# Half of the cross-attention weights turned through DRAM instead of by TensorE

## The chip, the cores and the metric

The kernel runs on one core of one Trainium2 chip. The metric is the device time of one execution in microseconds. A core has TensorE (matrix products, and transposes as products with an identity), VectorE, ScalarE, GpSimd, and SyncE, which here only issues DMAs; 16 DMA engines serve them.

## The reference

One post-norm decoder layer on 32 sequences of 56 tokens, 256 features, all in float32: self-attention, cross-attention to 1500 context positions, and a mixture of experts. The change lies in the middle part:

```
q = (text @ Wq), 16 heads of 128;  k, v = (ctx @ Wk), (ctx @ Wv), 8 heads, each used by two q heads
scores = q k^T / sqrt(128)                      # 16 x 56 x 1500 per sequence
attn = softmax(where(mask, scores, -inf))
x = layernorm(x + (attn v) @ Wo)
```

The kernel folds Wk into the queries and Wv into Wo (matrices M), so that the scores are products of the rotated queries with the context itself, and the weighted sum is one of context rows. A sequence (a *batch* of the attention) has 16 x 56 = 896 rows of weights, 7 *units* of 128 rows, and 1500 keys.

## The kernel before, in words

Phase A computes the self-attention and the rotated queries, phase C the experts; the change leaves both nearly as they are. Phase B is the cross-attention. Products are made exact to float32 by splitting each operand into a rounded part and a remainder (`_hi`, `_lo`, type fp32r) and adding three products: hi x hi, hi x lo, lo x hi.

Phase B goes over pairs of batches. The seven units of a batch stand in two slots, four units and then three; a slot has 12 *chunks* of 125 keys, and a pair has 48 steps, one per chunk. Per step every engine has its part, in an order written out by hand by step numbers:

- **fill** (TensorE L817 to L819): one third of a unit's scores, 128 x 500, into one of three score banks; VectorE (L983) adds the mask, takes the maximum and writes the row tile `p`; ScalarE (L901) takes exp of a whole unit of 1500 columns.
- **turn** (TensorE L831): the weighted sum needs the keys on the partitions, so each chunk of `p` (128 rows x 125 keys per unit) is turned into a PSUM bank, four transposes in an even slot, three in an odd one.
- ScalarE (L895) rounds the turned chunk to `pT_hi`, VectorE (L997) writes the remainder `pT_lo`.
- **weigh** (TensorE L850 to L852): three products of a chunk of context with `pT_hi` and `pT_lo`, 512 columns or 384, added up in an output bank over the 12 chunks.

Two batches' outputs are scaled by the reciprocal sums, rounded, and projected with M (L860, 48 products); then comes the layer norm. GpSimd splits queries, context and transposed context into hi and lo (L1099, L1101) and makes the mask's bias (L1110). SyncE loads `q_in`, `cT_in`, the mask and the context `c_in` for the batches ahead; ScalarE stores and loads the reciprocals. An engine does its instructions in order; a semaphore holds it where data or a buffer is missing. Matching rows of program and profile carry the same line number; the kernel's functions follow.

Of the kernel before, what the change touches and what calls it, by code (L numbers as in the profile page):

```python
# [26 lines left out]
ALU = mybir.AluOpType  # L27
# [21 lines left out]
CH = 12  # L49
CK = CTX // CH  # L50
FILLS = 3
FW = CTX // FILLS
ROWS = XH * S
UNITS = (4, 3)
SLOTS = 4
WIDE = UNITS[0] * 128
# [11 lines left out]
for width in (NT, EXPERTS * EXPERTS, 128, RP, RP, NT, NT * EXPERTS, 128):  # L68
# [8 lines left out]
Attention = namedtuple("Attention", "sync tensor scalar vector gpsimd edge tail q_split cT_split c_split fill_done fill_taken "  # L77
                       "first_batch_weighed weighed third_slot_turned all_lo projected z_taken y2_stored")
# [45 lines left out]
def phase_a(nc, D, semaphore, M_hi, M_lo, q_in, cT_in, ident, ident_loaded):  # L124
    with ExitStack() as ctx:
# [107 lines left out]
        def sync(sp, load_ahead):  # L233
# [56 lines left out]
            def store_last():  # L290
                store_q(NBLK - 1, range(PARTS))
                sp.wait_ge(y_stored, 16 * NPAIR)
                for part in range(PARTS):
                    sp.wait_ge(q_stored[part], 16 * NBLK)

            return store_last
# [331 lines left out]
def phase_b(nc, D, semaphore, edge, opening, M_hi, M_lo, q_in, cT_in, ident, const_loaded):  # L628
    with ExitStack() as ctx:
        def sb(name, shape, dt=F32):  # L630
            edge[name] = nc.sbuf_base
            return ctx.enter_context(nc.sbuf_tensor("b_" + name, shape, dt))

# [9 lines left out]

        oT = sb("oT", [128, XH, 2, S])
        oT_hi = sb("oT_hi", [128, XH, 2, S], F32R)
        oT_lo = sb("oT_lo", [128, XH, 2, S], F32R)
        y1_res = sb("y1_res", [PAIR, F])
# [4 lines left out]
        sb("spare", [128, 2480])  # L652
        pT_hi = sb("pT_hi", [CK, 3, WIDE], F32R)
        pT_lo = sb("pT_lo", [CK, 3, WIDE], F32R)
        p = [None, sb("p1", [128, UNITS[1], CTX])]
        rden_all = sb("rden_all", [128, 2, WIDE])
# [6 lines left out]
        c_in = sb("c_in", [CK, CH * CD])  # L663
        c_hi = sb("c_hi", [CK, 2, CH * CD], F32R)
        c_lo = sb("c_lo", [CK, 2, CH * CD], F32R)
        mask_in = sb("mask_in", [128, CTX], U8)
        mask_add = sb("mask_add", [128, 2, CTX], BF16)
        half = sb("half", [PAIR, 1])
        top = sb("top", [128, 2, UNITS[0], FILLS + 1])
        top_min = sb("top_min", [128, FILLS + 1])  # L670
        shift = sb("shift", [128, 2, UNITS[0]])
        den = sb("den", [128, 2, UNITS[0]])
        rden = sb("rden", [128, 2, UNITS[0]])
        p[0] = sb("p0", [128, UNITS[0], CTX])
        edge["end"] = nc.sbuf_base
# [3 lines left out]
        q_loaded, cT_loaded, c_loaded, mask_loaded = sem("q_loaded"), sem("cT_loaded"), sem("c_loaded"), sem("mask_loaded")  # L679
# [29 lines left out]
        def units(slot):  # L709
            return UNITS[slot % 2]  # L710
# [1454 lines left out]
```

## Time and profile before

| | |
|---|---|
| median of 3 runs | 1717.78 us (1717.73 to 1717.91) |
| span of the profiled execution | 1718.6 us |
| its own time outside the span | not given apart; the span is 0.8 us above the median |
| mean granted clock of TensorE | 0.994 of 2.4 GHz |
| DMA, mean over the span | 82 GB/s |

The span goes from the first to the last instruction of one profiled execution. A share of an engine is its busy time over the span. In the tables of stretches, DMA share is the mean busy share of the 16 DMA engines. In the chain of waits, followed back from the end, each piece is the time that TensorE (or another) spent as the last to be ready. Rows of instruction groups give the busy time in all and the mean duration of one in ns; a matmul's mean duration overlaps its neighbours, so for TensorE the chain's pieces tell the pace.

### The profile page before, as it was taken

The numbers are of one execution on the slowest core, as the hardware profiler recorded it, in microseconds if no ns is written. First come the engines' busy times: TensorE is split into PE (matmuls) and PEld (weight loads), VectorE is DVE, ScalarE is ACT, GpSimd is POOL, SyncE is SP. The second block draws the span as 40 slices with busy tenths as digits, with TensorE's granted clock in tenths as the row PEclk, the third lists the DMA queues.
The fourth block names the chain that finished last, engine by engine and source line by source line (L and its number), as shares of the span: only waits on it lengthen the run. The fifth ranks groups of instructions, "written<-read, shape, count | busy, mean of one in ns | idle before, by whom it ended". The sixth has DMA issues, their size and how long they took to land.

```text
span 1718.6 us, 28903 instructions
## 1 busy us (share of the span) xinstructions
PE 1685.0 (98%) x10034; PEld 1517.0 (88%) x10034; DVE 1221.3 (71%) x3377; ACT 937.2 (55%) x1717; POOL 664.6 (39%) x417
## 2 busy tenths in 40 slices
PE   7999999999999999999999999999999999999996
PEld 7998889898989898989898989989898989888985
DVE  5655676877787878777778777776878787756557
ACT  5444465656565656565656565565656565644543
POOL 1220344525243333333334343443525341355435
PEclk9999999999999999999999999999999999999998
DMA  5234643423141423333232323232324130431433
GB/s 197 81 132 130 193 95 78 70 68 81 54 97 41 90 44 88 48 86 68 62 68 63 68 63 68 70 66 77 74 61 89 52 57 12 112 114 40 121 90 95
DMA packets 102856, 140.29 MB, mean 82 GB/s; under 512 B 37022, under 2 KB 81728, under 8 KB 102592
## 3 DMA queue, kind: packets, MB, share of 16 engines
q1 hardware_dynamic: 60784, 115.47, 26.8%
q10 hardware_dynamic: 38912, 14.80, 4.0%
q0 software_dynamic: 3024, 8.26, 1.8%
q8 instruction: 79, 1.29, 0.4%
q14 instruction: 57, 0.47, 0.2%
HBM read 113.62 MB, written 24.89 MB: 81 GB/s over the span
## 4 chain that ended last, share of the span: by engine, by line
PE 93%; DVE 2%; issue 1%; ACT 1%; DMA 1%; POOL 0%; another core or an unknown queue 0%; POOLq 0%; SPq 0%; ACTq 0%; DVEq 0%
PE b_turn L831 17%; PE b_out L850 9%; PE b_out L851 9%; PE b_out L852 9%; PE b_score L817 9%; PE b_score L819 9%; PE b_score L818 9%; PE b_out L860 5%; PE a_bank L344 5%; PE c_gate L1513 2%; PE c_down L1540 1%; PE a_bank L370 1%; PE a_bank L395 1%; PE a_bank L424 1%; PE a_bank L417 1%
## 5 line engine op out<-in xcount | busy, mean ns | idle before, releaser
L895 ACT CAST b_pT_hi<-b_turn 125x512 fp32r<-125x512 f32 (+1 forms) x768 | 406.8, 530 | 543.0 <-PE b_turn L831 539.8
L997 DVE TENSOR_TENSOR b_pT_lo<-b_turn,b_pT_hi 125x512 fp32r<-125x512 f32 (+1 forms) x768 | 478.0, 623 | 259.7 <-ACT b_pT_hi L895 254.2
L983 DVE CUSTOM_DVE_ANT_0 b_p<-b_score,b_mask_add 128x500 f32<-128x500 f32 x672 | 451.9, 673 | 58.9 <-PE b_turn L831 24.4
L831 PEld LDWEIGHTS b_turn<-ident,b_p 128*125 128x125 f32 x2688 | 409.4, 186 | 55.2
L831 PE MATMUL b_turn<-ident,b_p 128*125 128x128 f32 x2688 | 418.1, 272 | 0.0
L901 ACT ACTIVATE b_p<-b_p,b_shift 128x1500 f32<-128x1500 f32 x224 | 347.5, 1551 | 2.1 <-DVE b_top_min L991 2.1
L850 PE MATMUL b_out<-b_pT_hi,b_c_hi 125*128 125x512 f32 (+1 forms) x768 | 346.5, 451 | 0.7 <-DVE b_pT_lo L997 0.6
L1135 POOL TENSOR_TENSOR b_oT_lo<-b_oT,b_oT_hi 128x896 fp32r<-128x896 f32 x32 | 67.6, 2112 | 624.5 <-ACT b_oT_hi L925 588.0
L851 PE MATMUL b_out<-b_pT_lo,b_c_hi 125*128 125x512 f32 (+1 forms) x768 | 280.9, 366 | 0.0
L852 PE MATMUL b_out<-b_pT_hi,b_c_lo 125*128 125x512 f32 (+1 forms) x768 | 280.5, 365 | 0.0
L817 PE MATMUL b_score<-b_cT_hi,b_q_hi 128*128 128x500 f32 x672 | 262.9, 391 | 0.0
L819 PE MATMUL b_score<-b_cT_hi,b_q_lo 128*128 128x500 f32 x672 | 260.2, 387 | 0.0
L818 PE MATMUL b_score<-b_cT_lo,b_q_hi 128*128 128x500 f32 x672 | 259.8, 387 | 0.0
L852 PEld LDWEIGHTS b_out<-b_pT_hi,b_c_lo 125*128 125x128 f32 x768 | 144.2, 188 | 17.9
L819 PEld LDWEIGHTS b_score<-b_cT_hi,b_q_lo 128*128 128x128 f32 x672 | 126.1, 188 | 25.8
L850 PEld LDWEIGHTS b_out<-b_pT_hi,b_c_hi 125*128 125x128 f32 x768 | 145.7, 190 | 1.5 <-DVE b_pT_lo L997 1.4
L851 PEld LDWEIGHTS b_out<-b_pT_lo,b_c_hi 125*128 125x128 f32 x768 | 145.9, 190 | 0.0
L818 PEld LDWEIGHTS b_score<-b_cT_lo,b_q_hi 128*128 128x128 f32 x672 | 128.1, 191 | 14.2
L817 PEld LDWEIGHTS b_score<-b_cT_hi,b_q_hi 128*128 128x128 f32 x672 | 126.2, 188 | 14.1
L1101 POOL TENSOR_TENSOR b_c_lo<-b_c_in,b_c_hi 125x1536 fp32r<-125x1536 f32 x32 | 111.9, 3497 | 2.7
L1101 POOL TENSOR_TENSOR b_cT_lo<-cT_in,b_cT_hi 128x1500 fp32r<-128x1500 f32 x31 | 106.3, 3428 | 2.6
L860 PE MATMUL b_out<-M_lo,b_oT_hi 128*112 128x256 f32 x256 | 71.8, 280 | 0.0
(250 smaller groups left out, 2402.1 us busy)
## 6 DMA issues: line engine op xcount, KB each, us to landing
cT_in<-in_ctxT SPq DMA_DIRECT2D x32, 750.0 KB, 9.8
b_c_in<-in_ctx SPq DMA_DIRECT2D x32, 750.0 KB
q_store<-a_fold_in_or_q_stage SPq DMA_DIRECT2D x16, 896.0 KB, 4.2
q_in<-q_store SPq DMA_DIRECT2D x32, 448.0 KB, 7.1
b_rden_all<-rden_store ACTq DMA_DIRECT2D x32, 256.0 KB, 3.6
b_rden_all<-rden_store ACTq DMA_DIRECT2D x32, 192.0 KB, 3.7
b_mask_in<-in_mask SPq DMA_DIRECT2D x32, 187.5 KB, 9.4
slot_store<-c_y2T SPq DMA_DIRECT2D x35, 128.0 KB, 1.7
```

The lines of the kernel that those rows point to most:

```text
L817: pe.matmul(out, q_hi[b][:, rows], cT_hi[b][:, keys], start=True, stop=False)
L818: pe.matmul(out, q_hi[b][:, rows], cT_lo[b][:, keys], start=False, stop=False)
L819: pe.matmul(out, q_lo[b][:, rows], cT_hi[b][:, keys], start=False, stop=True).then_inc(fill_done, 1)
L831: mm = pe.transpose(turn_bank[n % 3][0:CK, u * 128:(u + 1) * 128], p[slot % 2][:, u, c * CK:(c + 1) * CK], ident[:])
L850: pe.matmul(out, hi, pT_hi[:, n % 3, 0:w], start=(c == 0), stop=False)
L851: pe.matmul(out, hi, pT_lo[:, n % 3, 0:w], start=False, stop=False)
L852: pe.matmul(out, lo, pT_hi[:, n % 3, 0:w], start=False, stop=(c == CH - 1)).then_inc(pv_done, 1)
L895: act.copy(pT_hi[:, n % 3, 0:w], turn_bank[n % 3][0:CK, 0:w]).then_inc(hi_done, 1)
L901: act.activation(row, row, ACT.Exp, bias=shift[:, slot % 2, u:u + 1], scale=float(X_SCALE), accum_out=den[:, slot % 2, u:u + 1]).then_inc( ...
L983: dve.tensor_tensor_reduce(out=p[slot % 2][:, u, keys], in0=score_bank[j][:, 0:FW], in1=mask_add[:, b, keys], scale=1.0, scalar=-3.0e38, o ...
L997: dve.tensor_tensor(pT_lo[:, n % 3, 0:w], turn_bank[n % 3][0:CK, 0:w], pT_hi[:, n % 3, 0:w].bitcast(F32), ALU.subtract).then_inc(lo_done, 1)
L1101: pool.tensor_tensor(lo, src, hi.bitcast(F32), ALU.subtract).then_inc(done, 1)
```

## The change

Units are now worked by single batches: 24 steps (`STEPS = 2 * CH`) for one batch's seven units. The odd slot's three units are turned by TensorE as before. The four even units of a batch take another way:

1. VectorE (`turn_blocks`) turns the unit's 128 x 1536 values in 32 x 32 blocks into the one buffer `by_block`, at steps 5, 9, 13 and 17. It reads the row so that 32 keys (padded beyond 125) of each of 12 chunks and four quarters (`al`) come as blocks.
2. SyncE stores `by_block` to DRAM (`store_p`), 6144 B for each of 128 rows.
3. When a batch's four units are stored, SyncE fetches them (`load_keyed`): for each unit and each quarter `a` of its rows a band of 384 columns into `keyed`, with the keys on the partitions. The source is read as 4 quarters of keys x 32 x 384 values; the target is 128 partitions x 384 values. `keyed` is a single buffer; the fetch waits until the even products of the batch before are done.
4. ScalarE (`keyed_round`) rounds a chunk of 512 columns, GpSimd (`keyed_rest`) writes the remainder over `keyed`, and TensorE (`weigh_even`) multiplies, twelve chunks later than the odd units' products.

To make room, the remainders of the context and of the scaled output are written over their sources, `p0` holds three units, and the residual is loaded into `z`. The casts of `cT` and `c` go from GpSimd to ScalarE (`cT_round` at step 1, `c_round` at step 8). The projection is cut into four parts of 12 products. In phase C tiles move to other regions; two shared-expert weights are loaded only when the attention's products are done.

```diff
+        STEPS = 2 * CH
...
+        HI_AT = STEPS + 2
+        PV_AT = HI_AT + 2
+        BLOCKS_AT = (5, 9, 13, 17)
+        RDEN_AT, STORE_AT, LOAD_AT = (15, STEPS + 1), (16, STEPS + 2), (STEPS + 16, STEPS + 8)
+        SCALE_AT = (PV_AT + STEPS - 1, PV_AT + CH - 1)
+        ROUND_AT = SCALE_AT[0] + 1
...
+            def store_p(m, u):
+                sp.wait_ge(blocks_turned, EVEN * m + u + 1)
+                if m >= 2:
+                    sp.wait_ge(keyed_loaded, 16 * QUADS * EVEN * (m - 1))
+                sp.dma_start(D["p"][m % 2, u].rearrange("q a n -> q (a n)"),
+                             by_block[:].rearrange("q al b j -> q (al b j)")).then_inc(p_stored, 16)
+            def load_keyed(m, u):
+                if m:
+                    sp.wait_ge(pv_done, whole(m - 1))
+                sp.wait_ge(p_stored, 16 * EVEN * (m + 1))
+                for a in range(QUADS):
+                    sp.dma_start(keyed[:, QUADS * u + a, :],
+                                 D["p"][m % 2, u, 32 * a:32 * (a + 1)].rearrange("i al n -> al i n")).then_inc(keyed_loaded, 16)
...
+            for m in range(B):
+                if m >= 2:
+                    load_c(m)
+                if m:
+                    store_p(m, 0)
+                    for u in range(EVEN):
+                        load_keyed(m - 1, u)
+                if m + 2 < B:
+                    load_q(m + 2)
+                if m:
+                    store_p(m, 1)
+                store_p(m, 2)
+                if m + 2 < B:
+                    load_cT(m + 2)
+                    load_mask(m + 2)
+                store_p(m, 3)
...
-                for u in range(units(slot)):
-                    mm = pe.transpose(turn_bank[n % 3][0:CK, u * 128:(u + 1) * 128],
-                                      p[slot % 2][:, u, c * CK:(c + 1) * CK], ident[:])
+                for u in range(ODD):
+                    mm = pe.transpose(turn_bank[c % 3][0:CK, u * 128:(u + 1) * 128],
+                                      p[1][:, u, c * CK:(c + 1) * CK], ident[:])
...
+                pe.wait_ge(keyed_lo_done, CH * m + c + 1)
+                out, (hi, lo) = by_blocks(out_bank[0][:]), values(m, c)
+                own_hi = by_blocks(pT_hi[:, c % 3, :])
+                pe.matmul(out, hi, own_hi, start=(c == 0), stop=False)
+                pe.matmul(out, hi, keyed_chunk(keyed_lo, c), start=False, stop=False)
+                pe.matmul(out, lo, own_hi, start=False, stop=(c == CH - 1)).then_inc(pv_done, 1)
...
+            def keyed_round(m, c):
+                if c == 0:
+                    act.wait_ge(keyed_loaded, 16 * QUADS * EVEN * (m + 1))
+                act.wait_ge(pv_done, STEPS * m + CH + c - 2)
+                act.copy(by_blocks(pT_hi[:, c % 3, :]), keyed_chunk(keyed, c)).then_inc(hi_done, 1)
...
+            def turn_blocks(m, u):
+                dve.wait_ge(exp_done, PUNITS * m + u + 1)
+                dve.wait_ge(p_stored, 16 * (EVEN * m + u))
+                own = row(m, u)
+                keys = bass.AP(own.tensor, own.offset, [own.ap[0], [32, QUADS], [CK, CH], [1, 32]])
+                dve.transpose(by_block[:], keys).then_inc(blocks_turned, 1)
...
+            def keyed_rest(m, c):
+                pool.wait_ge(hi_done, STEPS * m + CH + c + 1)
+                pool.tensor_tensor(keyed_chunk(keyed_lo, c), keyed_chunk(keyed, c),
+                                   by_blocks(pT_hi[:, c % 3, :]).bitcast(F32),
+                                   ALU.subtract).then_inc(keyed_lo_done, 1)
...
+    D["p"] = nc.dram_tensor("p_store", (2, EVEN, 128, QUADS, ACROSS), F32, kind="Internal").ap()
```

TensorE, an even slot in the steady state: the scores of a fill (`b_score`), then one chunk, its turn (`b_turn`) and its products (`b_out`). Before:

```order
L817 MATMUL b_score2<-b_cT_hi0,b_q_hi0 128x500
L818 MATMUL b_score2<-b_cT_lo0,b_q_hi0 128x500
L819 MATMUL b_score2<-b_cT_hi0,b_q_lo0 128x500
L831 MATMUL b_turn1<-ident,b_p0 125x128 x4
L850 MATMUL b_out0<-b_pT_hi,b_c_hi 128x512
L851 MATMUL b_out0<-b_pT_lo,b_c_hi 128x512
L852 MATMUL b_out0<-b_pT_hi,b_c_lo 128x512
```

After, the same stretch of work (`b_keyed_over` is the remainder written over `keyed`, `b_c_raw1_over` that of the context over its source):

```order
L864 MATMUL b_score0<-b_cT_hi0,b_q_hi0 128x500 [waits b_fill_taken]
L865 MATMUL b_score0<-b_cT_lo0,b_q_hi0 128x500
L866 MATMUL b_score0<-b_cT_hi0,b_q_lo0 128x500
L912 MATMUL b_out0<-b_pT_hi,b_c_hi1 128x512 [waits b_keyed_lo_done]
L913 MATMUL b_out0<-b_keyed_over_50,b_c_hi1 128x512
L914 MATMUL b_out0<-b_pT_hi,b_c_raw1_over_52 128x512
```

The four transposes are gone; the first product waits for the remainder of the fetched chunk.

SyncE's queue, one batch. Before:

```order
L750 ISA [waits b_q_split]
L750 DMA q_in<-q_store 128x896
L756 ISA [waits b_cT_split]
L756 DMA cT_in<-in_ctxT 128x1500
L759 DMA b_mask_in<-in_mask 128x1500
L766 DMA b_c_in<-in_ctx 125x1536 [waits b_c_split]
```

After (`p_store` is the DRAM tensor of step 2; where rows are left out, the same four rows of `b_keyed` stand three times more, 16 fetches in all):

```order
L786 DMA b_c_raw0<-in_ctx 125x1536 [waits b_pv_done]
L792 DMA p_store<-b_by_block 128x1536 [waits b_keyed_loaded,b_blocks_turned]
L802 DMA b_keyed<-p_store 128x1x384 [waits b_p_stored,b_pv_done]
L802 DMA b_keyed<-p_store 128x1x384 x3
...
L772 DMA q_in<-q_store 128x896 [waits b_q_split]
L792 DMA p_store<-b_by_block 128x1536 [waits b_keyed_loaded,b_blocks_turned] x2
L776 DMA cT_in<-in_ctxT 128x1500 [waits b_cT_lo_done]
L781 DMA b_mask_in<-in_mask 128x1500 [waits b_mask_ready]
L792 DMA p_store<-b_by_block 128x1536 [waits b_keyed_loaded,b_blocks_turned]
```

Between the load of `c` and that of `q_in` stand a store and sixteen fetches; the stores of the second, third and fourth unit come behind them in the same queue.

VectorE, scores (`b_p`, `b_top`) and remainders (`b_pT_lo`). Before:

```order
L991 TENSOR_SCALAR b_top_min,b_shift<-b_top 128x4 [waits b_fill_taken]
L997 TENSOR_TENSOR b_pT_lo<-b_turn0,b_pT_hi 125x512 [waits b_hi_done]
L997 TENSOR_TENSOR b_pT_lo<-b_turn1,b_pT_hi 125x512 [waits b_hi_done]
L983 ISA b_p1,b_top<-b_score0,b_mask_add 128x500 [waits b_fill_done]
L983 ISA b_top 128x1
L997 TENSOR_TENSOR b_pT_lo<-b_turn2,b_pT_hi 125x512 [waits b_hi_done]
```

After, around the block transpose of one unit (step 9):

```order
L1067 ISA b_top 128x1
L1076 TENSOR_SCALAR b_top_min,b_shift<-b_top 128x4 [waits b_fill_taken]
L1091 TENSOR_TENSOR b_pT_lo<-b_turn1,b_pT_hi 125x384 [waits b_hi_done]
L1086 STREAM_TRANSPOSE b_by_block<-b_p0 128x1536 [waits b_p_stored,b_exp_done]
L1067 ISA b_p0,b_top<-b_score0,b_mask_add 128x500 [waits b_blocks_turned,b_fill_done]
L1067 ISA b_top 128x1
L1091 TENSOR_TENSOR b_pT_lo<-b_turn2,b_pT_hi 125x384 [waits b_hi_done]
```

The remainders have 384 columns; a transpose of 1536 columns stands between scores and waits until the store of the unit before has landed.

## Rows read from the trace of the kernel before

**Rows 1.** The page: busy us (share) x instructions, and the chain that ended last by line.
```profile
PE 1685.0 (98%) x10034; PEld 1517.0 (88%) x10034; DVE 1221.3 (71%) x3377; ACT 937.2 (55%) x1717; POOL 664.6 (39%) x417
...
PE b_turn L831 17%; PE b_out L850 9%; PE b_out L851 9%; PE b_out L852 9%; PE b_score L817 9%; PE b_score L819 9%; PE b_score L818 9%; PE b_out L860 5%; PE a_bank L344 5%; PE c_gate L1513 2%; PE c_down L1540 1%; PE a_bank L370 1%; PE a_bank L395 1%; PE a_bank L424 1%; PE a_bank L417 1%
```
**Rows 2.** Stretches: busy us and instructions by engine, granted clock, DMA share, GB/s.
```profile
174.60:256.50 81.90, 81.90 (x434) 72.80 (x435) 59.72 (x161) 42.97 (x69) 33.15 (x17) 0.98 0.58 143
256.50:1485.60 1229.10, 1229.10 (x7292) 1108.02 (x7291) 925.64 (x2656) 711.52 (x1171) 487.23 (x249) 1.00 0.31 69
1485.60:1519.70 34.10, 33.40 (x225) 30.44 (x224) 19.06 (x36) 19.96 (x36) 22.11 (x26) 1.00 0.09 22
```
**Rows 3.** The chain in order of time: start us, us, what; two projections.
```profile
949.65 5.62 PE b_out L860 x48
1031.60 5.62 PE b_out L860 x48
```
**Rows 4.** The chain, single chunks of four and of three units.
```profile
989.80 0.23 PE b_score L817
...
990.48 0.44 PE b_turn L831 x4
990.91 0.23 PE b_out L850
...
1301.38 0.33 PE b_turn L831 x3
1301.70 0.18 PE b_out L850
```
**Rows 5.** Groups of 256.5:1485.6: shapes, count | busy us, mean ns | idle before.
```profile
L983 DVE CUSTOM_DVE_ANT_0 b_p<-b_score,b_mask_add 128x500 f32<-128x500 f32 x630 | 423.7, 672 | 48.7 <-PE b_turn L831 23.6 <-PE b_score L819 6.5
...
L997 DVE TENSOR_TENSOR b_pT_lo<-b_turn,b_pT_hi 125x512 fp32r<-125x512 f32 x361 | 248.9, 689 | 180.2 <-ACT b_pT_hi L895 176.8
...
L997 DVE TENSOR_TENSOR b_pT_lo<-b_turn,b_pT_hi 125x384 fp32r<-125x384 f32 x360 | 200.1, 556 | 65.9 <-ACT b_pT_hi L895 64.6 <-issue 0.5
...
L895 ACT CAST b_pT_hi<-b_turn 125x384 fp32r<-125x384 f32 x360 | 171.3, 476 | 219.4 <-PE b_turn L831 219.4
...
L1101 POOL TENSOR_TENSOR b_c_lo<-b_c_in,b_c_hi 125x1536 fp32r<-125x1536 f32 x30 | 104.9, 3497 | 2.5
...
L1135 POOL TENSOR_TENSOR b_oT_lo<-b_oT,b_oT_hi 128x896 fp32r<-128x896 f32 x29 | 61.3, 2113 | 561.7 <-ACT b_oT_hi L925 561.7
...
L1099 POOL TENSOR_SCALAR b_c_hi<-b_c_in 125x1536 fp32r<-125x1536 f32 x30 | 44.5, 1483 | 0.0
...
L1099 POOL TENSOR_SCALAR b_cT_hi<-cT_in 128x1500 fp32r<-128x1500 f32 x29 | 42.1, 1452 | 0.0
```
**Rows 6.** Stretches of single transfers: c, c, storing q (phase A), cT.
```profile
1032.40:1038.40 6.00, 6.00 (x50) 5.85 (x49) 0.09 (x1) 0.71 (x2) 0.00 (x0) 1.00 0.29 116
950.50:956.50 6.00, 6.00 (x50) 5.83 (x49) 0.13 (x1) 0.75 (x2) 0.00 (x0) 1.00 0.31 122
...
76.70:78.70 2.00, 2.00 (x11) 1.73 (x10) 0.62 (x1) 0.28 (x1) 0.00 (x0) 1.00 1.01 333
...
1002.30:1005.10 2.80, 2.80 (x18) 2.51 (x17) 2.29 (x6) 1.64 (x4) 0.36 (x1) 1.00 0.93 330
```
**Rows 7.** DMA issues: out<-in, queue, count, KB each, median us to landing.
```profile
q_in<-q_store SPq DMA_DIRECT2D x32, 448.0 KB, 7.1
b_rden_all<-rden_store ACTq DMA_DIRECT2D x32, 256.0 KB, 3.6
b_rden_all<-rden_store ACTq DMA_DIRECT2D x32, 192.0 KB, 3.7
...
slot_store<-c_y2T SPq DMA_DIRECT2D x35, 128.0 KB, 1.7
```
**Rows 8.** Stretches where phase B begins.
```profile
171.00:174.60 3.60, 1.36 (x11) 0.91 (x10) 1.85 (x6) 1.91 (x4) 0.08 (x1) 1.00 0.79 195
174.60:178.10 3.50, 3.50 (x10) 3.09 (x11) 3.50 (x2) 1.77 (x2) 1.36 (x1) 0.51 0.80 287
178.10:182.00 3.90, 3.90 (x20) 3.53 (x20) 1.84 (x5) 0.54 (x1) 2.57 (x2) 1.00 0.97 332
```

More of the change, by code:

```diff
@@ new lines, in fills_at, with unit_ends, parity, behind @@
+        def fills_at(n):
+            return [f for f in range(PFILLS) if fill_step(f) == n]
+        def unit_ends(n, late):
+            return [f // FILLS for f in range(FILLS - 1, PFILLS, FILLS) if fill_step(f) + late == n]
+        def parity(u):
+            return (0, u) if u < EVEN else (1, u - EVEN)
+        def behind(m, n, at, count=1):
+            for k in range(3):
+                if at <= n + STEPS * k < at + count and 0 <= m - k:
+                    return m - k, n + STEPS * k - at
+            return None
@@ new lines, in units_behind, with row, whole, keyed_chunk @@
+        def units_behind(m, n, late, last):
+            ends = [] if last else [(m, u) for u in unit_ends(n, late)]
+            return ends + ([(m - 1, u) for u in unit_ends(n + STEPS, late)] if m else [])
+        def row(m, u):
+            return p[0][:, (EVEN * m + u) % EVEN_DEEP, :] if u < EVEN else p[1][:, u - EVEN, :]
+        def whole(m):
+            return STEPS * (m + 1)
+        def keyed_chunk(tensor, c):
+            return tensor[0:CK, :, 32 * c:32 * (c + 1)]
+        def by_blocks(ap):
+            return ap.rearrange("p (g j) -> p g j", j=32)
@@ L797, in sync @@
-            loads(1, first=True)
-            with sp.Fori(2, NPAIR) as i:
-                loads(i)
-            store(NPAIR - 2)
-            residual(NPAIR - 1)
+                load_mask(0)
+                load_c(0)
+            store_last_part, wait_stored = opening.sync(sp, load_ahead)
+            load_q(1)
+            load_cT(1)
+            load_mask(1)
+            load_c(1)
+            for part in range(len(opening.stored)):
+                if part >= 2:
+                    store_p(0, part - 2)
+                store_last_part(part)
@@ L854, in project @@
[L854 to L857 removed]
+                    if m == 0:
+                        pe.wait_ge(*opening.taken[1])
+                    else:
+                        pe.wait_ge(oT_done, OT_OPS * (2 * m - 1))
+                    pe.wait_ge(c_lo_done, m + 1)
+                pe.wait_ge(lo_done, CH * m + c + 1)
+                out, (hi, lo) = out_bank[1][:, 0:w], values(m, c)
+                pe.matmul(out, hi, pT_hi[:, c % 3, 0:w], start=(c == 0), stop=False)
@@ L861, in project @@
                                        start=(h == 0 and n == 0), stop=(h == XH - 1 and n == len(terms) - 1))
[L862 to L878 removed]
+                if part == parts - 1:
+                    mm.then_inc(proj_done, 1)
```

773 lines of the change are left out of this document (388 added, 385 removed).

## The prediction

> **What bounds the kernel now.** I read the page's busy shares first, then the chain of waits, then a table by stretches. TensorE is busy 98% of the span, the next engine 71% [rows 1]; the chain that ends last is TensorE for 93%, its largest line the turning L831 with 17% [rows 1]. In the attention proper, from 174.6 us to 1485.6 us, TensorE never idles: 81.90 of 81.90 us in the first pair of batches, 1229.10 of 1229.10 us in the fifteen that follow [rows 2]. A pair recurs every 81.95 us (the projection L860 starts at 949.65 and at 1031.60) [rows 3], so a batch takes 40.97 us. What this kernel does in the attention is the sum of TensorE's instructions; all else is hidden, DMA included (mean share 0.31, 69 GB/s) [rows 2].
>
> **What the change takes from TensorE.** In the chain a chunk of four units is turned in 0.44 us, one of three in 0.33 us [rows 4]. Twelve chunks of four per batch go: 12 x 0.44 = 5.28 us, and over 32 batches 169 us. The order shows nothing put in their place on TensorE: the even chunk's three products follow the scores directly. If all else stayed hidden, a batch would take 40.97 - 5.28 = 35.7 us.
>
> **What the other engines get, against 35.7 us a batch.** GpSimd is busy 487.23 us in thirty batches [rows 2], 16.2 us each. It gives the casts of c and cT to ScalarE (1.48 and 1.45 us) and gets twelve remainders of 512 columns. None is in the trace; 896 columns take 2113 ns and 1536 take 3497 ns [rows 5], 2.16 ns a column and some 180 ns besides, so 1.29 us each, 15.4 us a batch. That makes 28.7 us. It fits, and one remainder per step of 1.49 us (35.7 / 24) fits as well, barely; up to double is possible, since these tiles are cut into pieces of 32 columns, and would make GpSimd the bound at 44 us a batch. VectorE, busy 925.64 / 30 = 30.9 us a batch [rows 2], loses twelve remainders of 512 columns (689 ns [rows 5], 8.3 us) and gains four block transposes of 1536 columns. No row shows that operation. 384 and 512 columns take 556 and 689 ns [rows 5], 1.04 ns a column, which makes 1.75 us each, 7.0 us a batch; I bound it by 0.9 us (half) and 3.5 us (double) and take 1.75, the line through the nearest rows: 29.6 us. ScalarE, 711.52 / 30 = 23.7 us now [rows 2], gets the casts of cT and c, some 3 us more. By these values no engine becomes the bound by its work.
>
> **What the DMA gets.** Per batch and unit, one store of 128 rows x 6144 B (768 KB, four a batch) and four fetches of 128 x 1536 B (192 KB, sixteen a batch): 3 MB out and 3 MB back. The question is how many of the 16 DMA engines a fetch uses. In two windows in which only the load of c runs (125 rows), the DMA share is 0.29 and 0.31, with 116 and 122 GB/s; in a window of the load of cT (128 rows) it is 0.93 and 330 GB/s, and 1.01 and 333 GB/s where q is stored (128 rows) [rows 6]. 0.31 is 5/16: 125 rows are split by 5, and 128 by 16. So a transfer is cut along its outermost count into equal parts. The fetch of a band reads its source as 4 x 32 x 384 (al, i, n): the outermost count is 4, against 128 partitions on the other side. Cut the same way it runs on 4 engines.
> Here the Trainium skill has a rule that speaks against this change: "DMA: Bandwidth & Descriptors", section "Why a DMA increments its semaphore by 16 and not by 1", says that a hardware-issued transfer gets the largest number of engines, up to 16, that divides the slowest dimension of both sides. By that rule the trace's 0.31 for 125 rows is 5 engines, and agrees; a band gets 4. No transfer here has unlike counts on its two sides, so this half of the rule is not shown by any row. By the rule the sum is the one below; if only the 128 partitions counted, it would be that of the first rival.
> Four engines carry 786,432 B each per batch for the fetches. One engine moves 122 / 5 = 24.4 GB/s, 330 / (0.93 x 16) = 22.2 or 333 / (1.01 x 16) = 20.6 [rows 6]; I take 23.
>
> **The cycle of one batch.** SyncE's order is: store of unit 0, sixteen fetches of the batch before, q, store of unit 1, then store of unit 2. All go through one queue, so on the four engines the store of unit 1 stands behind the fetches. VectorE has one by_block buffer: its transpose of unit 2 (end of step 13) waits until unit 1 is stored, and behind it on VectorE, in order, stand all later scores; TensorE, with three score banks, stops at the fill of step 18. ScalarE's first rounding of the fetched bands (step 14) waits for the same fetches. So, from the issue of unit 0's store:
> 1. On each of the four engines: 2 x 49,152 B of stores, 786,432 B of bands, 28,672 B of q and as much of rden (448 KB each a batch [rows 7]), 942,080 B; at 23 GB/s 41.0 us. Issue and receipt 1.7 us (a 128 KB store lands in 1.7 us [rows 7]). The load of c, issued two steps earlier, is mostly through. 42.7 us.
> 2. Transpose of unit 2, 1.75 us, and the next score, 0.67 us [rows 5]: 2.5 us with the shift between them.
> 3. TensorE from step 18 to step 5 of the next batch. Its parts: a fill 3 x 0.225, products of 512 columns 3 x 0.23, of 384 3 x 0.175, a turn of three 0.33 [rows 4]. Five steps of 1.37, step 23 at GpSimd's 1.29, two of 1.37, two of 1.70, two of 1.53: 17.3 us.
> 4. From TensorE's end of step 5 to the end of the next unit 0's transpose: cast 0.48 and remainder 0.56 of three units [rows 5], transpose 1.75, less 0.5 beside TensorE: 2.3 us.
> 5. TensorE has then stood still for about 30 us. After it idled for 2.2 of 3.6 us, the trace shows a stretch of 3.5 us at granted clock 0.51, the lower of its two levels, 1.2 GHz, and 1.00 again after it [rows 8]. Half of such a stretch is lost at most, 1.7 us, part of it in waits: 1.2 us.
> Sum 66.0 us a batch, against 40.97.
>
> **The sum.** The profiled span is 1718.6 us, 0.8 above the median of the timed runs, 1717.8; what lies around the span is below what I can resolve here. Outside the attention's sixteen pairs 1718.6 - 1311.0 = 407.6 us stay. Batch 0 has no fetch: 35.7. Batches 1 to 31: 31 x 66.0 = 2046. At the end the last batch's fetch has no work beside it but some twelve light steps: 34 us of fetch and then the twelve chunks, against 34.1 us from the end of the pairs to the last projection now [rows 2]; I add 30 us, and 5 us for two shared-expert weights that the last stage now loads only when the attention's buffers are free (0 to 15). 407.6 + 35.7 + 2046 + 35 = 2524 us. For its own range the engine's rate gives 38.6 us (24.4) to 45.7 us (20.6) in term 1, the transpose -1.7 to +3.5 us, the queueing of c up to +5 us, term 5 0 to 1.7: with not all ends at once 60 to 75 us a batch, 2340 to 2805 us. GpSimd at double would lengthen term 3, in which eleven of its twelve remainders lie, by up to 11 us; with the low end of the rest that still is within the range.
>
> **The rivals.**
> First, and on the other side: the fetch is cut by its 128 partitions and uses all 16 engines. For it speaks that every 128-row transfer of the trace does; against it the 5 of 125, which show that counts decide. Then term 1 is (2 x 49,152 + 196,608 + 28,672) B at 20.6 GB/s, 15.7 us, + 1.7 = 17.4 us, and VectorE arrives at its wait after TensorE's steps 6 to 13, 7 fills of 0.675 and 8 x 0.855, 11.6 us. Of the 5.8 us late, TensorE's lead covers some 2: 39.7 us a batch, 407.6 + 35.7 + 31 x 39.7 + 10 = 1684 us. The point from which it decides: a batch gets slower than 40.97 us when the sixteen fetches take over some 11 us, that is with fewer than about 14 engines at this rate.
> Second: the fetches are hidden altogether and TensorE stays the bound: 407.6 + 32 x 35.7 + 10 = 1560 us. It needs the rival above and 6 us less of DMA.
> Third: four engines, but the waits overlap and only their occupancy counts. Per batch they carry 786,432 + 196,608 (stores) + 153,600 (c, a fifth of it) + 48,000 (cT) + 28,672 (q) + 12,000 (mask) + 28,672 (rden) = 1,253,984 B, at 23 GB/s 54.5 us: 407.6 + 35.7 + 31 x 54.5 + 35 = 2168 us. Against it: the by_block buffer is single and VectorE takes its work in order.
> That the change doesn't do what it says is excluded by the order.
>
> **How the numbers follow.** The forecast 2524 us has 0.76, the third rival 0.06, the first 0.11, the second 0.07. The range reaches from below the third rival to the upper end of the forecast's own: 2150 to 2820. Faster by over 0.2% (about what a measurement can tell here) are the first and second, less a little: 0.17; within 0.2% 0.01; slower 0.82.
>
> **What would show it.** Right: fetches of b_keyed landing over 30 us after issue; DMA share near 0.25 for most of a batch; VectorE idle some 28 us a batch before the transpose of by_block, released by the store of p; TensorE's share of the attention near 55%, L878 at three units only; a project line every 132 us. A half-speed clock after each stall would show term 5. Wrong: a DMA share of 0.8 or more while b_keyed is fetched, and a batch under 41 us. If the share is 0.25 and the time is not near 2524, a term of the cycle is mis-sized: the rate, or what stands behind what.

## The result, and the profile after

The changed kernel takes 2716.58 us (median of 4 runs, 2715.55 to 2726.51), the kernel before 1717.76 beside it: ratio 1.583 [1.580, 1.585]. The forecast was 2524 with a range of 2150 to 2820; the direction and the mechanism hold, and the size is 193 us short.

The page of the changed kernel: span, busy us (share) x instructions, then the chain that ended last, by engine and by line.

```profile
span 2713.7 us, 26254 instructions
...
PE 1691.3 (62%) x8498; PEld 1444.2 (53%) x8498; DVE 1189.1 (44%) x3134; ACT 1019.4 (38%) x1780; POOL 1038.2 (38%) x726
...
DMA 29%; SPq 26%; PE 17%; DVE 10%; ACT 4%; issue 3%; POOL 2%; DVEq 0%; ACTq 0%; POOLq 0%
SPq L802 24%; DMA p_store<-b_by_block 17%; DMA b_c_raw<-in_ctx 11%; DVE b_by_block L1086 5%; ACT b_p L971 2%; SPq L772 2%; PE b_out L912 2%; PE b_score L864 2%; PE b_score L866 2%; PE b_score L865 2%; DVE b_p L1067 2%; POOL b_keyed_over L1238 2%; PE b_turn L878 1%; PE c_gate L1632 1%; PE b_out L913 1%
```

TensorE was the chain for 93% [rows 1] and is now 17% of it. In its place stand SyncE's issuing of the fetches (L802, 24%), the landing of p's stores (17%) and, at 11%, the load of c, of which the prediction had said that it is mostly through.

The table of waits of the same kernel: who waited for whom, us in total, times, longest.

```profile
DVE b_by_block L1086 <- DMA p_store<-b_by_block: 867.3, 65, 28.5
PE b_out L912 <- POOL b_keyed_over L1238: 789.6, 100, 25.8
...
ACT b_pT_hi L964 <- DMA b_keyed<-p_store: 698.1, 31, 24.7
```

VectorE's transposes wait 65 times for the one by_block buffer. Some 800 of the 867.3 us fall before unit 2's transpose, up to 28.5 us each; the rest is a shorter wait before unit 3's, which the prediction does not have. ScalarE's first rounding of the bands waits 31 times, once a batch, up to 24.7 us. The waits at unit 2 and at the rounding are the two of the prediction's cycle.

Stretches of the changed kernel (busy us by engine, granted clock, DMA share, GB/s), as [rows 2]: the thirty batches' stretch of before, then one in which only bands are fetched, then the five microseconds behind an issue of c's load.

```profile
256.50:1485.60 1229.10, 701.59 (x3316) 589.94 (x3315) 506.00 (x1380) 449.07 (x701) 488.17 (x314) 0.79 0.48 127
...
1340.00:1345.00 5.00, 0.00 (x0) 0.00 (x0) 0.00 (x0) 0.00 (x0) 0.00 (x0) 0.50 0.27 100
...
1304.40:1309.70 5.30, 5.30 (x34) 4.97 (x33) 5.17 (x13) 4.21 (x7) 2.72 (x2) 1.00 0.19 22
```

TensorE is busy 57% where it was busy 100%. A band's fetch alone runs at share 0.27, 100 GB/s: four engines of sixteen, 25 GB/s each. All compute stands still there, and the clock is granted at its lower level (0.50, 1.2 GHz). The third row is the surprise: c's load is under way, and 22 GB/s move. In the kernel before, the same load moved 91 and 96 GB/s in the 5.3 us behind its issue (two batches), and 116 to 122 once it ran [rows 6].

SyncE's timeline over one batch (start us, us; a piece is a run of one kind of issue), and pieces of the chain of the same batch:

```profile
1238.53 0.33 SPq L792 DMA_DIRECT2D p_store<-b_by_block  x1
1238.96 32.83 SPq L802 DMA_DIRECT2D b_keyed<-p_store  x16
1271.83 1.83 SPq L772 DMA_DIRECT2D q_in<-q_store  x1
```
```profile
1273.76 10.63 DMA p_store<-b_by_block
...
1284.48 1.79 DVE b_by_block L1086
```

Sixteen issues hold SyncE for 32.83 us. The first two take 0.5 and 0.7 us, most of the later ones 1.86 us, about what one band's 196,608 bytes need at 100 GB/s; that an issue there waits for room in a full queue is read from this, not shown by a row. Unit 1's store, written behind them, lands at 1284.39, 45.9 us after unit 0's store was issued. Transposes of unit 2 start at 1213.27, 1284.48 and 1355.69: 71.2 us a batch, 71.4 over all 31, where the forecast had 66.0.

Groups of the page of after (busy us, mean ns | idle before) for the operations that no row of before showed:

```profile
L1238 POOL TENSOR_TENSOR b_keyed_over<-b_keyed,b_pT_hi 125x512 fp32r<-125x512 f32 x372 | 466.9, 1282 | 1051.2 <-ACT b_pT_hi L964 1051.2
...
L1086 DVE STREAM_TRANSPOSE b_by_block<-b_p 128x1536 f32<-128x1536 f32 x128 | 227.0, 1774 | 867.3 <-DMA p_store<-b_by_block 867.3
```

1282 ns against the 1.29 us forecast, 1774 against 1.75.

### The profile page after: what moved, and what is told of

It is laid out like the page before. It is cut to its first block, busy times and chain, and to the rows that moved or that the text cites. A ratio compares the mean times of both kernels' runs of the same rounds, so it can differ in the third digit from the quotient of the medians.

```text
span 2713.7 us, 26254 instructions
## 1 busy us (share of the span) xinstructions
PE 1691.3 (62%) x8498; PEld 1444.2 (53%) x8498; DVE 1189.1 (44%) x3134; ACT 1019.4 (38%) x1780; POOL 1038.2 (38%) x726
## 3 DMA queue, kind: packets, MB, share of 16 engines
q1 hardware_dynamic: 146800, 316.81, 41.5%
q10 hardware_dynamic: 38912, 14.80, 3.0%
## 4 chain that ended last, share of the span: by engine, by line
DMA 29%; SPq 26%; PE 17%; DVE 10%; ACT 4%; issue 3%; POOL 2%; DVEq 0%; ACTq 0%; POOLq 0%
SPq L802 24%; DMA p_store<-b_by_block 17%; DMA b_c_raw<-in_ctx 11%; DVE b_by_block L1086 5%; ACT b_p L971 2%; SPq L772 2%; PE b_out L912 2%; PE b_score L864 2%; PE b_score L866 2%; PE b_score L865 2%; DVE b_p L1067 2%; POOL b_keyed_over L1238 2%; PE b_turn L878 1%; PE c_gate L1632 1%; PE b_out L913 1%
## 5 line engine op out<-in xcount | busy, mean ns | idle before, releaser
L1238 POOL TENSOR_TENSOR b_keyed_over<-b_keyed,b_pT_hi 125x512 fp32r<-125x512 f32 x372 | 466.9, 1282 | 1051.2 <-ACT b_pT_hi L964 1051.2
L912 PE MATMUL b_out<-b_pT_hi,b_c_hi 125*128 125x512 f32 x384 | 186.1, 485 | 792.6 <-POOL b_keyed_over L1238 789.6
L1086 DVE STREAM_TRANSPOSE b_by_block<-b_p 128x1536 f32<-128x1536 f32 x128 | 227.0, 1774 | 867.3 <-DMA p_store<-b_by_block 867.3
L964 ACT CAST b_pT_hi<-b_keyed 125x512 fp32r<-125x512 f32 x384 | 218.8, 613 | 873.0 <-DMA b_keyed<-p_store 698.1
L1091 DVE TENSOR_TENSOR b_pT_lo<-b_turn,b_pT_hi 125x384 fp32r<-125x384 f32 x384 | 213.0, 556 | 294.0 <-ACT b_pT_hi L957 288.0
L957 ACT CAST b_pT_hi<-b_turn 125x384 fp32r<-125x384 f32 x384 | 179.8, 477 | 270.6 <-PE b_turn L878 266.3
L896 PE MATMUL b_out<-b_pT_hi,b_c_hi 125*128 125x384 f32 x384 | 167.7, 437 | 136.9 <-DVE b_pT_lo L1091 136.9
L878 PEld LDWEIGHTS b_turn<-ident,b_p 128*125 128x125 f32 x1152 | 193.9, 195 | 29.4
L878 PE MATMUL b_turn<-ident,b_p 128*125 128x128 f32 x1152 | 195.7, 280 | 0.0
L913 PE MATMUL b_out<-b_keyed_over,b_c_hi 125*128 125x512 f32 x384 | 167.1, 435 | 0.0
```

Source lines behind the costliest of these rows:

```text
L878: mm = pe.transpose(turn_bank[c % 3][0:CK, u * 128:(u + 1) * 128], p[1][:, u, c * CK:(c + 1) * CK], ident[:])
L896: pe.matmul(out, hi, pT_hi[:, c % 3, 0:w], start=(c == 0), stop=False)
L912: pe.matmul(out, hi, own_hi, start=(c == 0), stop=False)
L964: act.copy(by_blocks(pT_hi[:, c % 3, :]), keyed_chunk(keyed, c)).then_inc(hi_done, 1)
L1086: dve.transpose(by_block[:], keys).then_inc(blocks_turned, 1)
L1238: pool.tensor_tensor(keyed_chunk(keyed_lo, c), keyed_chunk(keyed, c), by_blocks(pT_hi[:, c % 3, :]).bitcast(F32), ALU.subtract).then_inc(k ...
```

## The experiments

Each ratio is given with its 95% interval against the kernel before (1717.5 to 1718.6 us). The time a batch is the mean distance of unit 2's transposes over batches 2 to 31, by which the changed kernel has 70.97 us.

**More engines for the same bytes.** The fetch in 4 transfers a batch, each into 32 partitions, with an outermost count of 32:

```
-  for a in range(QUADS):
-      sp.dma_start(keyed[:, QUADS*u + a, :], D["p"][m % 2, u, 32*a:32*(a+1)].rearrange("i al n -> al i n"))
+  sp.dma_start(keyed[32*u:32*(u+1), :, :], D["p"][m % 2, :, :, u].rearrange("v (a i) n -> i (v a) n", i=32))
```

> The same bytes in the same packets of 1536 B, fetched in four transfers per batch, one per quarter of 32 keys' partitions, whose outermost count is 32 on both sides, in place of sixteen with counts 4 and 128. Theory (a fetch is cut along its outermost count, 4 engines): all 16 engines carry it, the fetch takes some 9 us instead of the 32 us of the trace (1320 to 1352 us), DMA share 0.8 or more in it. The cycle was 71.2 us = 10.3 us from the store's issue to the first band + 32 + 3.6 + 25.2; it becomes 10.3 + 9 + 3.6 + 25.2 = 48 us, or less where the wait for c overlaps: 44 to 48 us, 1820 to 1950 us in all. Rival A (the pass through DRAM itself, 3 MB out and back with its waits, is the cost, whatever the number of engines): within 5% of 2717 us. Rival B (SyncE's issues are the cost, 24% of the chain): four issues instead of sixteen would help as much, so this run does not tell it from the theory; e2_eight does.

Measured 2320.5 us, 1.352 [1.349, 1.355], 58.9 us a batch. The count decides how many engines take part, but 16 of them bring less than four times the rate. The same cut in pieces of 8 partitions, so that 8 engines take part:

```
+  for k in range(QUADS): at = 8*k
+      sp.dma_start(keyed[32*u+at:32*u+at+8, :, :], D["p"][...].rearrange("v (a i) n -> i (v a) n", i=32)[at:at+8])
```

> Sixteen transfers of 192 KB per batch as before, same packets, but each takes 8 partitions and the source is read with an outermost count of 8. Theory: 8 engines, a fetch of 16 us instead of 32, DMA share near 0.5 in it, 55 us a batch, 2717 - 32 x 16 = 2205 us. Rival B (SyncE's sixteen issues at 1.86 us are the cost and not the engines): 2717 us, issues still 1.86 us apart. Rival A (the pass through DRAM): 2717 us.

Measured 2540.7 us, 1.479 [1.469, 1.489], 64.3 us a batch. The rivals of both runs, the pass through DRAM as such and SyncE's sixteen issues, had no change here, and are out. Stretches in which the bands are fetched, first of the 8-engine version, then of the 16-engine one (in the latter little else moves):

```profile
1190.00:1202.00 12.00, 8.01 (x43) 7.69 (x44) 5.87 (x14) 4.62 (x7) 3.48 (x1) 0.72 0.54 124
```
```profile
1260.00:1264.00 4.00, 2.06 (x6) 1.89 (x7) 2.67 (x3) 3.58 (x6) 3.00 (x1) 0.50 1.08 214
```

Share 0.27, 0.54, 1.08, but 100, 124, 214 GB/s: in the records of single packets between 600 and 1400 us, a packet of 1536 bytes takes 65 ns on the mean on 4 engines, 99 on 8 and 126 on 16. Both expectations had taken the rate per engine as given and were too low. From its first packet to its last, the fetch took 32.4 us in the changed kernel, 31.8 on 8 engines and 25.8 on 16 (means over batches 2 to 30). Of the 6.7 and 12.1 us a batch that the two versions win, some 6 come from the start: the first packet starts 3.9 and 4.0 us behind unit 0's store instead of 10.0, before c has landed. In the waits of the 16-engine version a new one is large:

```profile
ACT b_c_hi L1002 <- DMA b_c_raw<-in_ctx: 368.8, 30, 14.2
```

ScalarE casts c at step 8, in order before the exponentials of the units behind it, and c's load, issued at step 3 at the earliest, is not there: 12.3 us a batch. In the changed kernel the same wait was 229.7 us.

**c's load and the order of the queue.** In the changed kernel, c in two transfers of 112 and 13 rows:

```
-  sp.dma_start(c_raw[m % 2][:], D["ctx"][m])
+  for rows in (slice(0, 112), slice(112, CK)): sp.dma_start(c_raw[m % 2][rows, :], D["ctx"][m, rows, :])
```

> Only the load of c (125 rows, 5 engines) is cut into 112 and 13 rows. In the trace the first band starts 10.3 us after the store of unit 0 is issued, where 2.8 us were reckoned. Theory: c's 25 packets on each of the first five engines stand ahead of the fetch; with 7 + 1 packets the start comes some 5 us earlier, 66 us a batch, about 2560 us. Rival (c is through in time, the late start is the store of p or slow packets of all kinds): 2717 us within 15.

Measured 2641.2 us, 1.538 [1.535, 1.541]: 75 us less, between the two. c still took 11.4 to 11.7 us on the chain, so its five engines were only part of it. And unit 1's store ahead of the sixteen fetches:

```
   store_p(m, 0)
+  store_p(m, 1)
   for u in range(EVEN): load_keyed(m - 1, u)
```

> Only SyncE's order: the store of unit 1 stands ahead of the sixteen fetches, which so start at step 9 instead of 5, with c's load long done. Theory (what counts is the fetch's 32 us plus all the steps that can't go on beside it): VectorE's wait moves from unit 2's transpose to unit 3's and ScalarE's wait for the bands ends last; 36 us from unit 1's store to the bands + 29.6 us from step 14 to step 9 = 65.6 us a batch, 2540 us. Rival (the single by_block buffer behind the fetches is the cost by itself): once unit 1's store is ahead, most of the wait goes, under 2200 us; or, if the store of unit 2 only takes its place, 2717 us.

Measured 2897.1 us, 1.687 [1.683, 1.691], slower, and both expectations fell. VectorE's wait for the single buffer fell from 867.3 to 15.9 us, and still the time grew. SyncE waits for the transpose at step 9 before it issues any fetch, and that transpose stands behind ScalarE's wait for c: the first band starts 16.6 us behind unit 0's store instead of 10.0, and a batch takes 76.9 us. Its row of waits for the bands (the changed kernel has 698.1 and 24.7):

```profile
ACT b_pT_hi L963 <- DMA b_keyed<-p_store: 942.2, 31, 32.5
```

The fetch itself has to be early; the store's place behind it was the smaller evil.

**What slows c.** In the packet records of the changed kernel between 600 and 1400 us, a 6144-byte packet takes 234 ns in the median, but 918 ns on the mean when it starts 5 to 7 us behind an issue of the reciprocals' store, and up to 5.3 us singly. That store writes 512 and 384 pieces of 4 bytes, the second at step 2, right before c's load. One edit in the changed kernel makes it 128 pieces of 12 or 16 bytes, and leaves the order in DRAM unlike the one that the load expects, so that rows are scaled by other rows' sums:

```
-  D["rden"][m, par, 0:128*u].rearrange("(u q) -> q u", q=128)
+  D["rden"][m, par, 0:128*u].rearrange("(q u) -> q u", u=u)
```

> The changed kernel with one edit: the reciprocals of a batch go to DRAM as one piece of 16 or 12 bytes for each of 128 rows instead of 512 and 384 pieces of 4 bytes (their order in DRAM is then another, so the outputs are scaled by wrong denominators; the time alone counts). Theory: the 4-byte pieces slow every transfer beside and behind them for some microseconds (packets of 6144 bytes 234 ns each away from them, up to 2 us right behind them), c's load, issued just behind them, takes 15 us instead of 7, and the bands wait behind c: the load of c falls to 8 us, 5 to 7 us a batch come back, 2717 falls to 2500-2560. Rival: the slow packets come from something else that falls into the same steps: 2717 +- 15 and c still takes 15 us.

Measured 2571.2 us, 1.497 [1.494, 1.500]; 66.5 us a batch. The waits, and the five microseconds behind an issue of c's load:

```profile
ACT b_c_hi L1003 <- DMA b_c_raw<-in_ctx: 88.5, 30, 6.0
```
```profile
1235.60:1240.90 5.30, 5.30 (x34) 4.98 (x33) 5.17 (x13) 4.21 (x7) 2.72 (x2) 1.00 0.23 64
```

ScalarE waits 88.5 us for c, in the changed kernel 229.7; 64 GB/s move where 22 did; packets 5 to 7 us behind the issue take 237 ns instead of 918. The bytes differ by nothing that counts (14.80 MB on that queue in both), only the pieces. SyncE's sixteen issues take 28.6 us instead of 32.9 on the mean. The cycle of both kernels in parts (us, means over batches 2 to 30, from the packet records):

| | changed kernel | larger pieces |
|---|---|---|
| unit 0's store to the first band's packet | 10.0 | 5.0 |
| first to last band | 32.4 | 33.1 |
| last band to unit 2's transpose | 3.4 | 3.4 |
| from there to the next unit 0's store | 25.2 | 25.2 |

The whole gain is the earlier start of the bands. This is the theory's outcome, a little short of its range.

**Where the data lie.** Each unit stored in 4 transfers, by block of queries, so that it comes back in one transfer with an outermost count of 128:

```
+  for a in range(QUADS):
+      sp.dma_start(D["p"][m % 2, u, a].rearrange("(al i) n -> i al n", i=32), by_block[32*a:32*(a+1)]...)
...
+  sp.dma_start(keyed[:, QUADS*u:QUADS*(u+1), :], D["p"][m % 2, u].rearrange("a p n -> p a n"))
```

> The changed kernel with another layout in DRAM: each unit is stored in 4 transfers of 32 partitions, each block of queries apart, so that a unit is fetched back by one transfer whose outermost count is 128 (4 transfers a batch, all 16 engines, all 128 partitions at once, still 1536 bytes a packet). In the version with 4 transfers of 32 partitions the packets took 110 to 130 ns on 16 engines and 2320 us in all. Theory 1: those packets were slow because each transfer wrote to 32 partitions alone; with 128 partitions they take 65 to 80 ns, the fetch 10 us instead of 15, and the time falls to 2150-2220. Theory 2: 16 engines with packets of 1536 bytes end at some 200 GB/s however the partitions lie: 2320 +- 40, packets of 110 ns or more.

Measured 2296.3 us, 1.338 [1.336, 1.341]: by the time alone the second theory's number. Its own waits say otherwise:

```profile
ACT b_c_hi L1003 <- DMA b_c_raw<-in_ctx: 266.1, 30, 11.6
```

c is late here as well, 8.9 us a batch, and may cover what the fetch wins. The 16-engine version of before with c in two transfers:

> The version that fetches in 4 transfers of 32 partitions (2320 us), with c's load in two transfers of 112 and 13 rows, so that its rows go over 14 engines instead of 5. Theory: c's load, 20 us from issue to landing, is the wait that ScalarE's cast at step 8 has in that version (25% of the chain), because its packets stand in 5 queues; spread it takes 12 to 14 us and 4 to 6 us a batch go: 2130-2200. Rival: what holds c is the writes of other transfers that all engines share, and 2320 moves by no more than the 75 us that the same edit brought with 4 engines.

Measured 2149.3 us, 1.251 [1.246, 1.255]. 171 us for the edit that brought 75 with 4 engines; the theory's range. Then layout, split c and pieces of 12 or 16 bytes together:

> All three edits together: the layout with fetches of 128 partitions, c in two transfers, and the reciprocals stored in one piece a row (which leaves their order in DRAM wrong, the time alone counts). If the three costs are the three that hold the version with 4 transfers of 32 partitions (2320 us), they leave 1850-2000 us, still above the 1718 before, because store and fetch of 6.3 MB a batch at some 250 GB/s need 25 us of the 41 and the fetch can begin only when the last product of the batch before is done. If DRAM traffic as such bounds it, 2150 or more.

Measured 1925.0 us, 1.121 [1.119, 1.123], 46.4 us a batch, within the theory's range. A stretch of it in which the fetch runs, with part of q's load beside it:

```profile
1180.00:1187.00 7.00, 7.00 (x51) 6.73 (x50) 4.51 (x15) 1.70 (x4) 2.54 (x1) 1.00 1.05 395
```

395 GB/s, 342 of them bands, at 65 ns a packet in the median, against 214 for transfers into 32 partitions with the same packet size on the same 16 engines. So theory 1 of the layout was right on the packets. Whether the partitions or the order of the reads in DRAM does it, these runs don't part: the edit changes both. What is left on the chain is `DMA p_store<-b_by_block` with 29%, the single buffer; VectorE waits 319.8 us for it.

**Toward a version that beats both.** The layout and the split c stay. The reciprocals are turned by VectorE and stored in their right order as 28 pieces of 128 bytes, by_block has two buffers, and the fetch goes first.

```
-  act.dma_start(D["rden"][m, par, ...].rearrange("(u q) -> q u"), rden[:, par, 0:u])
+  dve.transpose(rden_t[:], rden[:])
+  for a in range(4): act.dma_start(D["rden"][m].rearrange("(u a j) -> a u j", a=4, j=32)[a], rden_t[32*a:32*a+7, :])
...
-  EVEN_DEEP = 3;  by_block = sb("by_block", ...)
+  EVEN_DEEP = 2;  by_block = [sb(f"by_block{k}", ...) for k in range(2)]
...
-  load_c(m); store_p(m, 0); load_keyed(m - 1, ...)      C_HI_AT = 8
+  load_keyed(m - 1, ...); load_c(m); store_p(m, 0)      C_HI_AT = 12
```

> A version meant to beat both, whose outputs are the reference's: units stored in 4 transfers by block of queries and fetched by transfers of 128 partitions; c in two transfers; the reciprocals of a batch turned by VectorE (one 128x32 transpose) and stored as 28 pieces of 128 bytes instead of 896 of 4; two buffers for the turned unit (the ring of even units one shorter), so that a transpose waits for the store two units back; and the fetch issued ahead of c's load and of unit 0's store, with c's cast moved from step 8 to step 12. Theory: what remains in the version with the first three (1925 us) is the wait of the transpose for the store (29% of the chain), which the second buffer ends, and the late start of the fetch (8.5 us at 65 ns a packet, wanted at step 14, free to begin at step 3). Then TensorE sets the pace with 12 turns of 4 units (5.3 us) fewer than before: 36 to 39 us a batch against 41, 1560 to 1660 us. Rival: DRAM traffic of 9.5 MB a batch, with stores in packets of 1536 bytes at 100 ns, still makes SyncE's queue late for the cast at step 14: 42 us a batch or more, 1750 or more.

Measured 1728.1 us, 1.0058 [1.0042, 1.0075]: between theory and rival. With fetches into 32 partitions instead:

> The same, but with the layout of the change: units stored in one transfer with packets of 6144 bytes, the fetch in 4 transfers of 32 partitions, whose packets took 110 to 130 ns in the first such version. If the fetch's speed decides (15 us against 8.5), this is slower by up to 5 us a batch, 1700 to 1800; if its 18 us of room cover it, it is as fast as the other within 20 us, or faster, since the stores are cheaper.

Measured 1910.4 us, 1.112 [1.110, 1.114], slower than its range: the fetch delays c behind it too (`DMA b_c_raw<-in_ctx` 24% of its chain). These two versions differ in the layout alone, with the stores that belong to it, which is worth 182 us here. The first of them with the old order of fetch, c and store, and c's cast back at step 8:

> The first of these with the old order: c's load and unit 0's store ahead of the fetch, c's cast at step 8. Theory: the fetch starts after unit 0's transpose at step 5 and after c, lands at about step 12 and is still just in time: within 40 us of the first. Rival: the late start is the larger part of what is left, and it takes back 3 us a batch or more: 90 us above the first.

Measured 1750.7 us, 1.019 [1.017, 1.021]: 22.6 us more, as the theory said. So of the 197 us between the version with three edits and the first of these, the early fetch with the later cast is 23, and 174 come with the second buffer (together with the reciprocals in 128-byte pieces; no run parts the two). The buffer's wait is gone: idle before the transpose, 867.3 us in the changed kernel and 319.8 in the version with three edits, is in the page of the first

```profile
L1092 DVE STREAM_TRANSPOSE b_by_block<-b_p 128x1536 f32<-128x1536 f32 x128 | 226.7, 1771 | 0.5 <-DMA p_store<-b_by_block 0.5
```

Its chain in order of time shows what is late next:

```profile
1071.12 11.74 DMA b_c_raw<-in_ctx
1082.88 1.49 ACT b_c_hi L1008
1084.44 3.48 POOL b_c_raw_over L1239
1087.92 1.22 POOL b_keyed_over L1250
```

c's load, cast and remainder stand ahead of the fetched keys' first remainder on GpSimd. The last run takes them away:

```
-  C_HI_AT = 12;  pool: c_rest(m) ahead of keyed_rest(m - 1, ...)
+  C_HI_AT = 18;  dve:  c_rest(m) at step 20
...
-  load_keyed(LAST, ...); load_piece(0..2)
+  load_piece(0..2); load_keyed(LAST, ...)
```

> The version of 1728 us with two more edits (outputs as in the reference). c's cast goes from step 12 to step 18 and its remainder from GpSimd, where it stood ahead of the fetched keys' remainders, to VectorE at step 20; and the last batch's fetch is issued behind the first three pieces of the next phase's weights instead of ahead of them. In the trace of that version each batch's chain runs from the release at step 3 through the load of c (11.7 us), its cast (1.4), its remainder on GpSimd (3.5) to the first remainder of the fetched keys; the loop takes 40.3 us a batch against 41.0 before, and the last score to the end 257 us against 234. Theory: with c off the chain TensorE alone sets the pace (94% busy there, 37.9 us): 38 to 39.5 us a batch, and the tail gives back 10 us: 1655 to 1700 us, 1 to 4% faster than before. Rival: VectorE, 76% busy and with 1.7 us more, or the fetch at step 14 holds the loop at 40 us a batch: 1710 to 1725, the same as before.

Measured 1716.1 us (median of 11), ratio 0.9995 [0.9984, 1.0005]: no difference from the kernel before, the rival's outcome. c has left the chain, but the batches alternate between 37 and 43 us in the distance of their first scores, and the keys' remainders on GpSimd take longer than in the version before it (1289 ns there):

```profile
L1252 POOL TENSOR_TENSOR b_keyed_over<-b_keyed,b_pT_hi 125x512 fp32r<-125x512 f32 x372 | 515.2, 1412 | 272.6 <-ACT b_pT_hi L966 268.2
```

They are 10% of its chain. The trace shows which ones slowed: 31 of the 372, one a batch, take 2.77 to 2.80 us, all others 1.29 on the mean, and each slow one runs beside the remainder of c that this version moved to VectorE. One such pair, GpSimd's and VectorE's:

```profile
576.00 2.79 POOL L1252 TENSOR_TENSOR b_keyed_over<-b_keyed,b_pT_hi 125x512 fp32r<-125x512 f32 x1
```
```profile
575.25 2.41 DVE L1181 TENSOR_TENSOR b_c_raw_over<-b_c_raw,b_c_hi 125x1536 fp32r<-125x1536 f32 x1
```

In all of these 31 batches VectorE's subtraction ends 1.6 us after the GpSimd instruction that was running when it began, and the slow one on GpSimd ends 1.1 us after VectorE's. It looks as if each waited until the other was done; no run takes the overlap away, so the cause is read from these times alone. GpSimd loses 1.5 us a batch by it. What makes the batches alternate stays open. TensorE is given 5.3 us less to do a batch; 1.0 of it is seen in the loop (39.95 us from first score to first score over all batches, 40.91 before). The tail takes most of that back: 254 us from the last score to the end, 235 before.

## Why the prediction was right, and where its size was off

**The count of engines: right.** A source with an outermost count of 4 runs on four engines though its other side has 128 partitions: 0.27 of the share, 100 GB/s. The Trainium skill's rule (page "DMA: Bandwidth & Descriptors", section "Why a DMA increments its semaphore by 16 and not by 1") is here shown for unlike counts too, and the first and second rivals are out.

**The waits: right.** VectorE at unit 2's transpose and ScalarE at step 14 wait where the prediction put them. The third rival, 54.5 us a batch of occupancy alone, is out: 71.4.

**Term 1 was mis-sized, 42.7 us forecast and 45.9 measured in this batch, and the part of it that failed is "the load of c, issued two steps earlier, is mostly through".** c was issued at 1304.38 and landed at 1319.28, unit 0's store was issued at 1309.71, and the first band's packets start at 1320: 10.3 us behind the store, where the prediction's bytes give 3.4 us (49,152 and 28,672 B at 23 GB/s). The bands themselves then take 32 us, 2.2 less than reckoned, since an engine moves 25 GB/s and not 23; what follows them takes 3.6 instead of 5.1. The range had "the queueing of c up to +5 us", but for c's bytes, not for single packets of up to 5.3 us.

**Outside term 1** the cycle was forecast with 23.3 us and takes 25.2 (1284.48 to 1309.71). The step left out is a second wait for the single buffer. Unit 3's transpose stands still until unit 2's store has landed, and then takes its own time; the prediction goes from unit 2's transpose straight to the next score. The two pieces on the chain:

```profile
1286.29 4.08 DMA p_store<-b_by_block
...
1290.47 1.78 DVE b_by_block L1086
```

Only 1.9 of these 5.9 us are missing in the sum, so that terms 2 to 5 together were some 4 us too large elsewhere; where, no run parts. ScalarE's wait for c at step 8, 229.7 us in 30 waits, 7.7 us each, is another step that the prediction lacks, but it lies between unit 0's store and unit 2's transpose, beside term 1: with the small writes in larger pieces it falls to 88.5 us, and the 25.2 us stay.

With the 4-byte pieces gone a batch takes 66.5 us, within 0.5 of the forecast's 66.0. That is partly luck: term 1 is then 41.5 us against 42.7, and the rest 25.2 against 23.3. Of the 5.4 us a batch that the forecast lacked (5.0 over batches 2 to 31), 4.4 are shown to be the small writes.

**The sum.** 31 x 5.4 = 167 of the 193 us lie in the cycle. The other 26 lie outside it, where the forecast had added 35 us for the tail. Part of that is seen there: the last sixteen fetches are issued from 2437.9 to 2468.4, the next phase's weights stand behind them in SyncE's queue, and TensorE idles meanwhile:

```profile
2460.00:2480.00 20.00, 0.00 (x0) 0.00 (x0) 0.00 (x0) 0.00 (x0) 0.84 (x2) 0.50 0.46 150
```

**The prices of the new work** (transpose 1774 ns, remainder 1282 ns) were right, and neither engine became the bound. **The clock** was granted at 0.79 on the mean over the attention, not the 1.2 us a batch of term 5 alone; since TensorE waits 43% of that time, its cost is not separate from the waits here, and no run parts it.

**The first rival's price was wrong where its mechanism was tried.** It gave 1684 us for 16 engines. Its own sum slips too: 35.7 + 5.8 - 2 is 39.5 and not 39.7, and it leaves out the reciprocals' 28,672 B an engine that term 1 counts, 1.4 us a batch at its rate. The runs gave 2320 with transfers into 32 partitions, as packets there take twice the time, and c's load and the single buffer held much of the rest. Only with the layout, c, the reciprocals and the buffer all mended is the time down at 1728.

## What to carry to other kernels

Count the engines of a transfer by the outermost count of both sides, and lay the intermediate tensor out in DRAM so that the way back has 128 there. Then list, for each transfer that moves to a busier step, what else is issued in the same microseconds: a store of a few hundred 4-byte pieces is nothing in bytes, and cost 4.4 us a batch here. A single buffer that is emptied through a queue shared with long transfers needs a second copy, but not first: with the slow fetch, taking its wait away by another order made the kernel slower, and with the fast one the second copy was part of 174 us. And when work moves from one engine to another, look at what runs beside it there: with a subtraction beside it on VectorE, GpSimd's took 2.78 us instead of 1.29.

## What the hardware showed unexpectedly

- Small writes slow others: 6144-byte packets at 918 ns on the mean 5 to 7 us behind the issue of 384 or 512 writes of 4 bytes, 237 when the same values went in pieces of 12 or 16 bytes.
- The same packet size, 1536 bytes, took 65 ns on 4 engines, 99 on 8 with transfers into 8 partitions, 126 on 16 with transfers into 32, and 65 on 16 engines when each transfer wrote 128 partitions from another layout in DRAM: 100, 124, 214, 395 GB/s.
- Sixteen issues in a row of transfers on 4 engines held SyncE for 32.83 us, most of them 1.86 us each.
- VectorE's subtraction of 125x1536 took 2454 ns on the mean (2106 to 2886) where GpSimd took 3503; it ended 1.6 us after GpSimd's instruction beside it, and GpSimd's next of 125x512 took 2.78 us instead of 1.29.
